# The opening stage of a non-local attention kernel, rewritten: two load queues, other engines for constants and weights, other banks for the values of image 0

## The reference

```python
C = 256; CQK = C // 8
xf = x.reshape(B, Cc, N)                                   # N = 1024
q = jnp.einsum('oc,bcn->bon', Wq, xf) + bq[None, :, None]  # 32 x 1024
k = jnp.einsum('oc,bcn->bon', Wk, xf) + bk[None, :, None]
v = jnp.einsum('oc,bcn->bon', Wv, xf) + bv[None, :, None]  # 256 x 1024
scores = jnp.einsum('bqi,bqj->bij', q, k)                  # 1024 x 1024
attn = jax.nn.softmax(scores, axis=-1)
out = jnp.einsum('bcj,bij->bci', v, attn)
return out.reshape(B, Cc, W, H) + x
```

## Time and profile before

| | us |
|---|---|
| median of 3 runs | 178.03 |
| lowest, highest | 176.54, 178.3 |
| the profiled execution | 178.07 |
| its span, first to last instruction | 175.9 |
| TensorE busy in the span | 167.4 (95%) |
| VectorE, ScalarE, GpSimd busy | 135.8, 112.2, 32.1 |

### The profile page before, as it was taken

How to read it: one execution, slowest core, us unless ns; L and a number is a source line. 1 busy time by engine, 2 the same in 40 slices (tenths; PEclk the granted TensorE clock), 3 DMA queues, 4 the chain that set the end, 5 groups by cost and what they waited for, 6 DMA issues and landing times.

```text
span 175.9 us, 2460 instructions
## 1 busy us (share of the span) xinstructions
PE 167.4 (95%) x812; PEld 133.9 (76%) x812; DVE 135.8 (77%) x223; ACT 112.2 (64%) x200; POOL 32.1 (18%) x33
## 2 busy tenths in 40 slices
PE   7998878999999999999999999999999999999992
PEld 2766856677889798887889798888889898876881
DVE  4658998867989998856989998857982997876353
ACT  6577786657887483847887484845686565745410
POOL 3008825000223020000223020000222020002410
PEclk9999999999999999999999999999999999999999
DMA  4942266006410202025310302026400221003003
GB/s 109 343 159 90 54 229 230 12 23 162 161 48 0 89 20 99 0 61 143 143 45 0 95 32 87 2 60 148 155 29 0 91 77 46 0 0 121 0 0 119
DMA packets 8044, 14.44 MB, mean 82 GB/s; under 512 B 992, under 2 KB 2528, under 8 KB 8032
## 3 DMA queue, kind: packets, MB, share of 16 engines
q1 hardware_dynamic: 7968, 14.29, 25.6%
q0 software_dynamic: 64, 0.00, 0.0%
HBM read 4.59 MB, written 4.19 MB: 50 GB/s over the span
## 4 chain that ended last, share of the span: by engine, by line
PE 79%; issue 1%; DVE 1%; ACT 0%
PE acc L741 33%; PE acc L749 15%; PE slot L617 15%; PE st L726 8%; PE slot L665 6%; PE acc L745 1%; PE st L713 1%; DVE o_sb L551 1%; ACT dump L355 0%; DVE w_hi L532 0%
## 5 line engine op out<-in xcount | busy, mean ns | idle before, releaser
L741 PE MATMUL acc<-w_hi,v_hi 128*128 128x512 f32 x128 | 51.3, 400 | 0.0
L741 PE MATMUL acc<-w_hi,v_lo 128*128 128x512 f32 x128 | 50.5, 395 | 0.0
L385 ACT ACTIVATE w_full<-st 128x512 f32<-128x512 f32 x64 | 37.7, 596 | 19.9 <-PE st L726 19.9
L310 POOL TENSOR_TENSOR w_lo<-w_full,w_hi 128x512 fp32r<-128x512 f32 x16 | 21.3, 1331 | 122.8 <-ACT w_full L385 103.7
L355 ACT ACTIVATE dump<-slot,negmax 128x1024 f32<-128x1024 f32 x29 | 32.4, 1118 | 12.8 <-DVE negmax L504 12.1
L749 PE MATMUL acc<-w_lo,v_hi 128*128 128x512 f32 x120 | 38.4, 396 | 0.0
L504 DVE TENSOR_REDUCE negmax<-slot 128x1 f32<-128x1024 f32 x29 | 35.3, 1218 | 2.9 <-PE slot L665 2.6
L541 DVE TENSOR_TENSOR w_lo<-w_full,w_hi 128x512 fp32r<-128x512 f32 x48 | 34.1, 709 | 3.8
L532 DVE CAST w_hi<-w_full 128x512 fp32r<-128x512 f32 x52 | 22.2, 426 | 14.7 <-ACT w_full L385 14.1
L741 PEld LDWEIGHTS acc<-w_hi,v_hi 128*128 128x128 f32 x128 | 24.2, 189 | 5.7 <-issue 0.4
L741 PEld LDWEIGHTS acc<-w_hi,v_lo 128*128 128x128 f32 x128 | 24.2, 189 | 5.2
(11 more groups left out here) (88 smaller groups left out, 185.3 us busy)
## 6 DMA issues: line engine op xcount, KB each, us to landing
out<-o_sb SPq DMA_DIRECT2D x7, 512.0 KB, 2.8
x_sb<-x SPq DMA_DIRECT2D x3, 1024.0 KB, 6.3
k_b<-k_a SPq DMA_DIRECT2D x8, 192.0 KB, 2.5
q_b<-q_a SPq DMA_DIRECT2D x8, 192.0 KB, 2.4
x_sb<-x SPq DMA_DIRECT2D x4, 256.0 KB, 4.4
k_a<-qk_parts SPq DMA_DIRECT2D x6, 128.0 KB, 2.3
q_a<-qk_parts SPq DMA_DIRECT2D x6, 128.0 KB, 2.3
out<-o_sb SPq DMA_DIRECT2D x2, 256.0 KB, 2.1
```

The source lines that it names most:

```text
L310: nc.gpsimd.tensor_tensor(w_lo[:, j % RING, :], w_full[:, j % RING, :], w_hi[:, j % RING, :].bitcast(fp32), ALU.subtract).then_inc(w_split ...
L385: nc.scalar.activation(w_full[:, j % RING, :], st[:, j % 2, :], ACT.Exp).then_inc(exp_done, 1)
L741: nc.tensor.matmul(acc[:, c, :], v[:, j, ch], w_hi[:, r, :], start=(j == 0 and v is v_hi), stop=False)
```

## The change

Nothing of the turns' order changes, save who makes the high and low parts of the first image's weight tiles. In the opening stage:

- SyncE issues quarters 0 and 1 of image 0, `wv` and image 1; ScalarE's queue issues `wqk` and quarters 2 and 3, ahead of its table load.
- `wqk_hi` goes from ScalarE to VectorE. `wv_hi`, `eye_r`, the high parts of q (both halves) and the ones in `k_b` go to GpSimd (the `ones` tile and VectorE's fill of it are gone).
- TensorE's products on zeros: 14 of 256 columns ahead of the projections, two of 256 between the quarters, 14 of 128 behind them.
- Scores 1, 2, 4, 5 and the values have other banks; the values now lie in the four halves of `slot`. The order on TensorE, ScalarE and VectorE behind the first four scores is another.
- Weight tiles 0 to 3 of image 0 get their high part from ScalarE (before: tile 0), and GpSimd splits tile 2 in place of tile 0 there.
- GpSimd prepares the last quarter of image 1 only when the shifts are made.
- Counting of semaphores is rewritten without an effect on what waits for what.

```diff
-    CUT_BY_ACT = (0, 9, 11)
-    SPLIT_BY_POOL = (0, 9, 11, 13)
+    def cut_by_act(n):
+        return n % PER in ((0, 1, 2, 3, 9, 11) if n < PER else (0, 9, 11))
+    def split_by_pool(n):
+        return n % PER in ((2, 9, 11, 13) if n < PER else (0, 9, 11, 13))
...
-        FIRST_HOME = {0: flat(acc), 1: slot[0][:, :], 2: flat(st), 3: flat(acc), 4: slot[1][:, :], 5: slot[0][:, :]}
+        FIRST_HOME = {0: flat(acc), 1: flat(st), 2: slot[0][:, :], 3: flat(acc), 4: slot[0][:, :], 5: slot[1][:, :]}
+        FIRST_V = (slot[1][:, cols(1)], slot[0][:, cols(0)], slot[0][:, cols(1)], slot[1][:, cols(0)])
...
 @block.sync
-            sp.dma_start(wqk[:, :, :], wqk_t.rearrange("(t p) m -> p t m", p=P)).then_inc(wqk_in, DMA)
-            for i in range(4):
+            for i in range(2):
                 sp.dma_start(x_sb[:, 0, :, quarter(i)], x_v[0, :, :, quarter(i)]).then_inc(x0_in[i], DMA)
...
 @block.gpsimd
-            pool.wait_ge(wcut, 2)
-            nc.gpsimd.tensor_tensor(wv_lo[:, :, :], wv[:, :, :], wv_hi[:, :, :].bitcast(fp32),
-                                    ALU.subtract).then_inc(wv_split, 1)
+            pool.wait_ge(eye_made, 2)
+            nc.gpsimd.tensor_copy(eye_r[:, :], eye[:, :]).then_inc(eye_cut, 1)
+            pool.wait_ge(eye_cut, 1)
+            nc.gpsimd.memset(k_b[SHIFT:K_B, :].bitcast(fp32), 1.0).then_inc(ones_put, 1)
...
+            def put_q_hi(h):
+                pool.wait_ge(q_put, h + 1)
+                nc.gpsimd.tensor_copy(q_a[2 * CQK:3 * CQK, cols(h)],
+                                      q_a[0:CQK, cols(h)].bitcast(fp32)).then_inc(q_hi_put, 1)
...
+            pool.wait_ge(x0_split, 4)
+            pool.wait_ge(wv_in, DMA)
+            nc.gpsimd.tensor_copy(wv_hi[:, :, :], wv[:, :, :]).then_inc(wv_cut, 1)
+            pool.wait_ge(wv_cut, 1)
+            put_q_hi(0)
+            pool.wait_ge(q_hi_put, 1)
+            nc.gpsimd.tensor_tensor(wv_lo[:, :, :], wv[:, :, :], wv_hi[:, :, :].bitcast(fp32),
+                                    ALU.subtract).then_inc(wv_split, 1)
             for i in range(3):
                 prepare_x1(i)
-            for j in range(AHEAD):
-                split_w(0, j)
+            pool.wait_ge(x1_split, 3)
+            put_q_hi(1)
+            pool.wait_ge(q_hi_put, 2)
+            pool.wait_ge(shift_ready, 1)
             prepare_x1(3)
...
 @block.scalar
+            act.dma_start(wqk[:, :, :], wqk_t.rearrange("(t p) m -> p t m", p=P)).then_inc(wqk_in, DMA)
+            for i in range(2, 4):
+                act.dma_start(x_sb[:, 0, :, quarter(i)], x_v[0, :, :, quarter(i)]).then_inc(x0_in[i], DMA)
             act.preload_act_table_set("natural_log_exp_and_others")
-            act.wait_ge(consts, 2)
-            nc.scalar.activation(k_b[SHIFT:K_B, :], ones[SHIFT:K_B, :], ACT.Copy).then_inc(ones_put, 1)
-            act.wait_ge(wqk_in, DMA)
-            nc.scalar.activation(wqk_hi[:, :, :], wqk[:, :, :], ACT.Copy).then_inc(wcut, 1)
...
+            for h in range(2):
+                cut_qk(0, h, FIRST_LOW)
+                put_k_hi(h)
             for t in range(TH):
                 sum_exp(0, t, True)
             log_sums(0, 0)
             cut_v(0, 0, True)
             cut_v(0, 1, True)
             put_rows(0, 0)
+            exp(0)
+            exp(1)
             cut_v(0, 2, True)
             cut_v(0, 3, True)
-            exp(0, 0)
-            sum_exp(0, TH, True)
-            exp(0, 1)
-            sum_exp(0, TH + 1, True)
+            for t in range(TH, TH + 2):
+                sum_exp(0, t, True)
...
 @block.vector
             shifts(0, 0)
-            for i in range(4):
-                split_v(0, i, True)
-                if i == 1:
-                    row_max(0, TH, True)
+            split_v(0, 0, True)
+            split_v(0, 1, True)
+            cut_w(0)
+            split_w(0)
+            cut_w(1)
+            split_w(1)
+            split_v(0, 2, True)
+            row_max(0, TH, True)
+            split_v(0, 3, True)
             row_max(0, TH + 1, True)
...
 @block.tensor
-                    if t in (4, 5) and h == 0:
-                        pe.wait_ge(v_split, t - 3)
+                    if t in (4, 5) and h == 0:
+                        pe.wait_ge(v_split, t - 1)
...
+            keep_busy(14, QUARTER)
             for i in range(4):
                 first_project_qk(i)
-            keep_busy(WAIT_PRODUCTS)
+                if i < 3:
+                    keep_busy(2, QUARTER)
+            keep_busy(14, P)
             for t in range(3):
                 first_scores(t)
             pe.wait_ge(wv_split, 1)
-            for t in range(2):
-                v_tile(0, t, True)
+            first_v(0)
             first_scores(3)
-            pe.wait_ge(rowsum_ready, 2)
-            for t in range(2, 4):
-                v_tile(0, t, True)
             pe.wait_ge(rowsum_ready, 3)
-            for t in range(4, 6):
-                v_tile(0, t, True)
-            pe.wait_ge(rowsum_ready, 4)
-            v_tile(0, 6, True)
+            first_v(1)
+            first_v(2)
+            pe.wait_ge(q_put, 2)
+            first_v(3)
             rows(0, 0, True)
+            scores_t(0)
+            scores_t(1)
             first_scores(TH)
-            v_tile(0, 7, True)
-            scores_t(0, 0, 0)
             first_scores(TH + 1)
-            pe.wait_ge(v_split, 3)
-            scores_t(0, 0, 1)
-            pe.wait_ge(v_split, 4)
```

## The result

| | before | changed |
|---|---|---|
| median, us | 178.09 (176.54 to 178.3, 4 runs) | 186.25 (185.51 to 188.05, 4 runs) |
| ratio | 1 | 1.0493, 95% interval 1.0392 to 1.0593 |
| profiled execution, us | 178.07 | 185.66 |
| its span, us | 175.9 | 183.4 |

A forecast was written before the change was run, and what follows sets the result against it. TensorE was taken to bound the kernel, so time follows its start on weight tile 1. +5.2 (R to tile 1) - 0.5 (T to R) - 0.4 (T) - 0.3 (gap) = +4.0 on 178.07: 182.0 us, range 180.4 to 185.6.

The forecast's parts named there:

- the point to beat: TensorE's start on the products of weight tile 1 in the kernel before: 28.89 + 0.32 = 29.21 us.
- T to R: First projection's end to first row maximum: GpSimd takes a 0.63 us copy, 2.25 us instead of 2.77, 0.5 gained.
- R to the products of tile 1: First row maximum to weight tile 1: late values and serial waits make 15.23 us into 20.4, 5.2 more.
- The sum: Whole kernel: +5.2 - 0.5 - 0.4 - 0.3 = +4.0 us on 178.07, giving 182.0 us.
- rival B: Same chain, but TensorE's clock falls in the new idle time: +2.9 us, about 184.9 us; chance 0.25.
- A: Likeliest case: the forecast chain with the clock high from about 10 us on, 180.7 to 183.3 us; chance 0.58.
- T: End of the first projection's last product: 10.5 us (9.2 to 11.7) instead of 10.89, 0.4 us gained.
- the missing wait: TensorE's 0.32 us idle before 32.88 in the kernel before, which could vanish: 0.3 us gained.
- The gain at the shifts: Last shift instruction 0.16 us instead of 1.13 without GpSimd overlap: 1 us gained, lost because `rows` stands behind the values.
- R: Start of the first row maximum, 13.66 us in the kernel before; later steps are counted from it.
- Rival C: Loads set the projection's end and land much earlier: 3.5 us gained, 179.0 us; chance 0.07, 0.03 for faster.
- Rival D: Chain right, but some more link late: one wait of 0.6 to 1.5 us per step, 183.5 to 185.5; chance 0.07.

The follow-up runs named there:

- a_values_first: Changed kernel with ScalarE's high parts and VectorE's low parts of values 2 and 3 put back ahead of exponentials 0, 1 and maximum 4: 180.06 us, ratio 1.0153.
- b_two_queues: Kernel before with the changed kernel's loads on two queues (SyncE and ScalarE), nothing else: 179.49 us, ratio 1.0102.
- a_warm_again: The same kernel as a_warm, run once more for its trace: 186.24 us.
- a_filler: Changed kernel without the six products on zeros between the quarters of the first projection: 186.0 us.
- a_warm: Changed kernel with 18 products of 512 columns on zeros added on TensorE, 12 ahead of scores 4, 6 ahead of scores 5: 183.88 us, ratio 1.0338.
- a_hold: Changed kernel, but SyncE issues `wv` and image 1 only when quarter 3 of image 0 has landed: 184.6 us.
- c_hold: c_merge with before's products on zeros and two load queues, `wv` waiting for quarter 1 and image 1 for quarter 3: 175.41 us, ratio 0.987.
- b_shift: Kernel before, with GpSimd waiting for the shifts before it prepares the third quarter of image 1: 176.0 us, ratio 0.992.
- c_merge: Changed kernel's sharing of constants, weights and q high parts, with before's load queue, banks, orders and weight tiles; 14 + 14 small zero products: 176.19 us, ratio 0.9908.

## Why the prediction was right or wrong, point by point

- **What bounds the kernel, and the point to beat: right.** From 50 to 90 us both kernels show the same table, and the 7.51 us at the projection behind tile 1 are the difference of the spans.
- **T to R: right.** 2.23 us for 2.25. Taking one 0.63 us copy off ScalarE gave 0.5, because VectorE's low part was the next to be late.
- **R to the products of tile 1, the mechanism: right up to scores 5, and shown** by the releasers in the trace and by a_values_first. Up to `scores_t(0)` the steps are right to 0.1 us. Scores 6 were released as forecast only with the clock held; in the changed kernel TensorE itself was late. The stretch measured 22.74 us for 20.4: 1.7 of the 2.3 us are the clock, the other 0.65 are links that I priced too low, on TensorE (36 value products 4.4 us instead of 4.3) and between `rows` and tile 1 (11.86 us instead of 11.3 with the clock held).
- **The clock: the step that failed.** The sum took the high level throughout, a cost of nothing, and gave the fall (rival B) a chance of 0.25. It fell behind scores_t(1) in each of the four traces with the chain and unfilled gaps. All sixteen timed executions of these kernels have a mean granted clock of 0.963 to 0.979, and none of before is below 0.988 (one of b_two_queues has 0.980, so a mean alone is not proof). The rival's price was 2.9 us; measured with the clock held it is 1.9 by the traces, 2.4 by the medians. With the rival in place of A, the forecast would have been 184.9. The Trainium skill ("TensorE: Matmul & The Clock Gate", section "What's actually happening") says that idling brings the low clock back, and the trace agrees: after the last product at 24.9 us TensorE stood idle, and from 27 us on the granted clock is 0.50. I had that and the 3.2 us empty stretch side by side and trusted that no row of before showed a fall. Before had no idle stretch like it, so that was no evidence.
- **T: the step with the wrong sign, the second that failed.** Forecast -0.4, measured +0.8. The measured 11.67 lies at the upper bound (9.2 to 11.7), and four traces with two queues have 11.4, 12.0, 12.2 and 13.2 (a_values_first, a_warm_again, a_filler, a_warm), three of them beyond it. In the profiled execution quarter 1 came 0.9 later (cut at 7.14 instead of 6.24), and behind it TensorE, mostly at the low level, waits for nothing more. In the other traces with two queues quarter 1 came at 5.6 to 6.3, as forecast, and T is late all the same; in a_warm_again and a_filler TensorE waits for quarter 3 (0.34 and 2.13 us). Quarter 0 did not come earlier: its issue moved from 1.38 to 0.75 us, its cut from 4.14 to 4.79. I had taken the later quarters for early enough. Quarter 3 came at 9.4 to 10.1, and at 8.1 in b_two_queues. The loads row already said that the engines were 98% busy; with them full, moving image 1 up can only move something else back. The forecast weighed a saving of 0 to 1.2 us in issue time and left out that reordering has a price. a_hold shows the sharing as the cause of the late quarter 3. How much of the 0.8 us each quarter bears isn't settled, since the clock's level in the first 10 us differs from one execution to the next, and one queue again gave back 0.6 us of T but no time clear of the scatter.
- **The sum.** 182.0 + 1.9 (clock) + 1.2 (T) + 0.5 (the links priced too low, less 0.16 that the missing wait gave beyond its 0.32) + 0.1 (outside the span) = 185.7, the profiled 185.66. The median lies 0.6 higher still. Two errors on one side carried the time out of the range; the range had the clock or a late T, not both. So the direction was right and the size half of what was measured: +4.0 us against +8.2.
- **The gain at the shifts: right that it was lost in the changed kernel, mis-sized in itself.** In the kernel before it is worth 1.0 us from R, not 0.4: I followed one reader of the late instruction and not the split behind it on the same engine.
- **Rival C (loads much earlier)** was ruled out rightly. It needed T below 8.2. With all quarters in hand by 7.2 and high-level products, a_hold has T = 9.95, so that landing alone would not have got there. That the landing itself did not come earlier is the sharing, which this rival had not counted.
- **Rival D (some more link late)** did not come up as one wait of 0.6 us or more. Behind tile 1 there is no wait over 0.3 us.

## What to carry to other kernels

When instructions of a hand-ordered kernel wait for banks, write the chain out through all engines: here the high parts of two value tiles, placed behind four exponentials on ScalarE, and their low parts, placed behind tile splits and a maximum on VectorE, cost 4.1 us on TensorE, though ScalarE had been idle while it could have made them. Price every new idle stretch of TensorE a second time, for the clock: here the clock fell behind the empty stretch in all four traces that left it open, and in three traces also at the value products, behind a stretch in which TensorE worked half the time or less. And when the DMA engines are full, issuing earlier reorders the transfers and does not speed them up. Holding back what is wanted later helped here, until the held image came so late that its preparation lay over the shifts (c_hold).

## What the runs showed of the hardware

- The clock's level in the opening is not a property of the kernel. In the kernel before, 256-column products of the first projection lie 0.21 us apart until 10.3 us; with b_shift's edit, which touches nothing there, they lie 0.12 us apart inside a pair from 6.64 on:

```profile
4.99 0.77 PE L641 MATMUL slot<-x_hi,wqk_hi 128*128 128x256 f32 x2
...
6.64 0.51 PE L641 MATMUL slot<-x_hi,wqk_hi 128*128 128x256 f32 x2
6.99 0.40 PE L645 MATMUL slot<-x_hi,wqk_lo 128*128 128x256 f32 x2
```

  T differs by 1.6 us between the two, and before's own executions scatter over 2.7 us (176.5 to 179.2); that the one is the cause of the other is argued, not shown. The landing of the first quarter scatters too: in six traces with one queue it is cut between 4.14 and 5.82 us (before and c_merge).
- The granted-clock column shows 1.00 over those 0.21 us products of before, and a lower value only where the clock had risen before and fell again: 0.76 from 5 to 10 us in a_warm, whose pairs of products take 0.39 us at 6.99 and 0.65 at 9.58. In the first microseconds the distance of two products is the better witness.
- A GpSimd subtraction of 1.28 us held a VectorE instruction on 128 x 4 elements for 1.13 us instead of 0.16, and waiting it out made the kernel 0.8% faster. In c_hold such a subtraction held another one for 0.85 us. Maxima over PSUM beside the same GpSimd work took 1.21 us, as without it.
